# An AdaLN block with a Mamba scan and a mixture of experts: z of batch 0 in the y banks, the second norm's normalising step on ACT, and three groups of readout transposes at other places

## The reference

```
h  = layernorm(x) * (1 + ca) + sa
xz = h @ in_proj.T ;  xs, z = split(xz)                # 256 + 256 channels
u  = silu(causal_conv4(xs) + conv_b)
dt, Bm, Cm = split(u @ x_proj.T)                       # 8, 16, 16
delta = softplus(dt @ dt_w.T + dt_b)
h[t] = h[t-1] * exp(delta * A) + delta * u * Bm        # 16 states per channel
y    = sum_n h * Cm + u * D
x  = x + ga * ((y * silu(z)) @ out_proj.T)
h  = layernorm(x) * (1 + cb) + sb
x  = x + gb * (shared_expert(h) + top2_of_8_experts(h))  # gelu MLPs, 128 -> 256 -> 128
```

## Time and profile before

| | us |
|---|---|
| median of three executions | 722.49 |
| the profiled execution, its own time | 720.62 |
| its span, first to last instruction | 718.9 |
| PE busy | 612.3 (85%) |
| DVE busy | 583.7 (81%) |
| ACT busy | 496.8 (69%) |
| POOL busy | 322.4 (45%) |
| PE idle before L509, ended by ACT L821 | 15.8 |
| DVE idle before scans L1088, all | 28.1 |
| ACT idle before gelus L911, ended by PE L608 | 17.9 |

### The profile page before, as it was taken

How to read it: one execution, slowest core, us unless ns; L and a number is a source line. 1 busy time by engine, 2 the same in 40 slices (tenths; PEclk the granted TensorE clock), 3 DMA queues, 4 the chain that set the end, 5 groups by cost and what they waited for, 6 DMA issues and landing times.

```text
span 718.9 us, 9754 instructions
## 1 busy us (share of the span) xinstructions
PE 612.3 (85%) x3662; PEld 478.7 (67%) x3662; DVE 583.7 (81%) x669; ACT 496.8 (69%) x894; POOL 322.4 (45%) x172
## 2 busy tenths in 40 slices
PE   6637378999899999999999989999999858996797
PEld 4214255779566966778577956796687747795576
DVE  4494999989998999979997999899997999694300
ACT  2666742989578975899388947898399915871464
POOL 1043456445644555536543564455543654463000
PEclk9859559999999999999999999999999969997899
DMA  6413244313532244123431343223422243300000
GB/s 210 197 41 135 104 144 136 119 59 136 183 116 83 108 147 146 64 113 118 165 118 58 144 176 121 78 81 133 172 68 109 118 146 118 133 1 16 0 1 16
DMA packets 26369, 77.80 MB, mean 108 GB/s; under 512 B 2817, under 2 KB 17234, under 8 KB 18130
## 3 DMA queue, kind: packets, MB, share of 16 engines
q1 hardware_dynamic: 25842, 76.75, 29.7%
q10 hardware_dynamic: 480, 0.43, 0.2%
HBM read 74.55 MB, written 2.62 MB: 107 GB/s over the span
## 4 chain that ended last, share of the span: by engine, by line
PE 49%; ACT 23%; DVE 18%; issue 7%; POOL 2%; DMA 1%; DVEq 0%; POOLq 0%; ACTq 0%
PE psum L638 9%; PE psum L482 9%; DVE state L1088 9%; ACT decay L781 7%; PE psum L509 7%; ACT gT_mix L877 6%; DVE psum L1079 4%; PE psum L606 4%; PE psum L607 4%; PE psum L608 4%; ACT h L911 3%; PE psum L623 2%; PE psum L648 2%; PE psum L527 2%; POOL state L407 1%
## 5 line engine op out<-in xcount | busy, mean ns | idle before, releaser
L407 POOL TENSOR_TENSOR state<-state,bc 128x1024 f32<-128x1024 f32 x128 | 302.3, 2362 | 318.8 <-DVE psum L1079 317.7
L1088 DVE TENSOR_TENSOR_SCAN state<-decay,psum 128x1024 f32<-128x1024 f32 x128 | 292.2, 2283 | 28.1 <-PE psum L482 9.4
L781 ACT ACTIVATE decay<-delta,a_neg 128x511 f32<-128x511 f32 x256 | 166.9, 734 | 11.0 <-DVE state L1088 10.3
L482 PE MATMUL psum<-ident,state 128*128 128x128 f32 x1024 | 143.1, 288 | 31.3 <-POOL state L407 31.3
L482 PEld LDWEIGHTS psum<-ident,state 128*128 128x128 f32 x1024 | 124.4, 149 | 56.5 <-POOL state L407 41.7
L1079 DVE TENSOR_TENSOR psum<-bc,du 128x1024 f32<-128x1024 f32 x128 | 157.5, 1231 | 4.8 <-DVE state L1088 0.5
L638 PE MATMUL psum<-down_w,h 128*128 128x128 f32 x1024 | 125.3, 276 | 0.0
L638 PEld LDWEIGHTS psum<-down_w,h 128*128 128x128 f32 x1024 | 119.2, 192 | 6.1 <-issue 6.1
L911 ACT ACTIVATE h<-psum,vec 128x512 f32<-128x512 f32 x144 | 97.6, 688 | 19.1 <-PE psum L608 17.9
L877 ACT ACTIVATE gT_mix<-psum,w 128x128 f32<-128x128 f32 x256 | 74.6, 397 | 20.3 <-PE psum L648 12.9
L509 PE MATMUL psum<-h_sb,conv_in_wT 128*128 128x512 f32 x128 | 60.9, 623 | 15.8 <-ACT z_silu L821 15.8
(11 more groups left out here) (141 smaller groups left out, 621.9 us busy)
## 6 DMA issues: line engine op xcount, KB each, us to landing
bc<-bc_rows SPq DMA_DIRECT2D x64, 1024.0 KB, 4.8
x_sb<-_attn_hidden_states_dram SPq DMA_DIRECT2D x9, 256.0 KB, 2.8
out_dram<-out_sb SPq DMA_DIRECT2D x8, 256.0 KB, 2.4
x<-_attn_hidden_states_dram SPq DMA_DIRECT2D x7, 256.0 KB, 3.0
h<-in_L_ffn_rw_dram SPq DMA_DIRECT2D x1, 1024.0 KB
bc_rows<-rows SPq DMA_DIRECT2D x8, 64.0 KB, 3.6
h<-in_L_wmod_dram ACTq DMA_DIRECT2D x1, 384.0 KB
h<-in_L_attn_in_proj_w_dram SPq DMA_DIRECT2D x1, 256.0 KB, 4.6
```

Source lines behind the costliest of these rows:

```text
L407: pool.tensor_tensor(state[:, u % STATE_RING, :, :], state[:, u % STATE_RING, :, :], bc[:, pair % BC_RING, 1, first:first + NU, :], ALU.mu ...
L482: last = nc.tensor.matmul(Y[q][:, t * P:(t + 1) * P], state[:, u % STATE_RING, s, t * P:(t + 1) * P], ident[:, :], start=False, stop=(u in ...
L781: last = nc.scalar.activation(decay[:, r, s, 1:L], delta[:, b.p, q, 1:L], ACT.Exp, scale=a_neg[:, q, k:k + 1])
L1088: nc.vector.tensor_tensor_scan(state[:, u % STATE_RING, :, :].rearrange("p n t -> p (n t)"), decay[:, u % DECAY_RING, :, :].rearrange("p n ...
```

## The change

Six edits, in the order of the program:

1. z of batch 0 is computed in the prologue, into the banks Y (`z_bank`), around x_proj; its silu follows at once. It was computed into A after dt, and its silu stood at the end of slot 0's share before it, behind 12 decay instructions. The convolution of batch 1 now waits for softplus_abs of batch 0 where it waited for z's silu.
2. Still in front of slot 0, ACT's `h_rows` of batch 1 stands ahead of the decays of batch 0; in slot 0 PE runs y_start and y_add 0 ahead of x_proj.
3. `x1hat` goes from DVE to ACT: out = x * rstd + shift, by four activations. POOL makes shift = -mean * rstd in two more instructions of 128x4 behind make_rstd (`make_shift`).
4. On ACT, x1hat and h2_rows stand ahead of softplus_exp with its table load; they stood behind it.
5. The decays of unit 6 stand ahead of the silu table's load at the head of the slot; they stood behind h2_rows.
6. On PE, y_add 2 takes the place of seven of the twelve keep_busy transposes behind x1_transpose; y_add 3 stands behind the last up step, y_add 4 behind weights_transpose.

The rest is a constant of -1, a tile and two semaphores.

```diff
@@ -247,6 +250,10 @@

         block = ctx.enter_context(nc.Block())

+        def z_bank(n, half):
+
+            return Y[half] if n.i == 0 else A[half]
+
         def skip_rows(b):

             return gT_mix[:, :].rearrange("p (q t) -> p q t", q=Q) if b.i == 0 else skip
@@ -396,6 +404,14 @@
                 pool.wait_ge(eps_added, b.i + 1)
                 pool.tensor_tensor(rstd[:, which, :], rstd[:, which, :], minus_half,
                                    ALU.pow).then_inc(done, 1)
+
+            def make_shift(a):
+                pool.tensor_tensor(shift[:, :], mean_var[:, 1, :, 0], minus_one,
+                                   ALU.mult).then_inc(minus_mean, 1)
+                pool.wait_ge(minus_mean, a.i + 1)
+                pool.wait_ge(rstd2_done, a.i + 1)
+                pool.tensor_tensor(shift[:, :], shift[:, :], rstd[:, 1, :],
+                                   ALU.mult).then_inc(shift_done, 1)

             def readout(b, u, paced=True):
                 pair, q, first = unit(u)
@@ -416,6 +432,7 @@
                         readout(b, u)
                     if a and u == 2:
                         make_rstd(1, stats2_done, rstd2_eps, rstd2_done, a)
+                        make_shift(a)
                     if m and u == 5:
                         make_rstd(0, stats_done, rstd_eps, rstd_done, m)

@@ -463,6 +480,8 @@

                 if not (isinstance(b.i, int) and b.i == 0):
                     pe.wait_ge(gT_done, b.i)
+                else:
+                    pe.wait_ge(zs_done, 2)
                 pe.wait_ge(skip_done, Q * b.i + Q)
                 for q in range(Q):
                     for t in range(NT):
@@ -503,18 +522,24 @@
                     pe.wait_ge(h_done, n.i + 1)
                     if not (isinstance(n.i, int) and n.i < 3):
                         pe.wait_ge(mixmul_done, DOWNS * (n.i - 2))
-                    elif n.i > 0:
+                    elif n.i == 2:
                         pe.wait_ge(zs_done, 2 * n.i)
+                    elif n.i == 1:
+                        pe.wait_ge(sp_abs, Q)
                 for k in range(KC):
                     last = nc.tensor.matmul(A[q], conv_in_wT[:, q, k, :], h_sb[:, k:k + L],
                                             start=(k == 0), stop=(k == KC - 1))
                 last.then_inc(conv_done, 1)

             def z_proj(n, half):
-                pe.wait_ge(sp_abs, Q * n.i + half + 1)
+                if n.i > 0:
+                    pe.wait_ge(sp_abs, Q * n.i + half + 1)
+                else:
+                    pe.wait_ge(set_ev, EV_PROJ)
+                bank = z_bank(n, half)
                 for t in range(2):
                     rows_of = KC - 1 + (2 * half + t) * P
-                    last = nc.tensor.matmul(A[half][:, t * DI:(t + 1) * DI],
+                    last = nc.tensor.matmul(bank[:, t * DI:(t + 1) * DI],
                                             h_sb[:, rows_of:rows_of + P],
                                             z_wT[:, :], start=True, stop=True)
                 last.then_inc(z_done, 1)
@@ -668,13 +693,20 @@
                 if a:
                     y_add(a, UN - 3)
                     y_add(a, UN - 2)
+                if b and not a:
+                    y_start(b)
+                    y_add(b, 0)
+                if n and n.i == 0:
+                    z_proj(n, 0)
                 if n:
                     x_proj(n)
+                if n and n.i == 0:
+                    z_proj(n, 1)
                 if a:
                     y_add(a, UN - 1)
                 if a:
                     g_transpose(a, n)
-                if b:
+                if b and a:
                     y_start(b)
                 if a:
                     out_proj(a)
@@ -684,9 +716,9 @@
                     att_transpose(a)
                 if n:
                     dt_proj(n, 1)
-                if b:
+                if b and a:
                     y_add(b, 0)
-                if n:
+                if n and n.i > 0:
                     z_proj(n, 0)
                     z_proj(n, 1)
                 if b:
@@ -694,15 +726,20 @@
                 if a:
                     keep_busy(a, n, 14)
                     x1_transpose(a)
-                    keep_busy(a, n, 12)
+                if b:
+                    y_add(b, 2)
+                if a:
+                    keep_busy(a, n, 5 if b else 12)
                     router(a)
-                for k in range(M_UP):
-                    if a:
+                    for k in range(M_UP):
                         up(a, n, k)
-                    if b and k in (2, 8, 14):
-                        y_add(b, 2 + (k - 2) // 6)
+                if b:
+                    y_add(b, 3)
                 if a:
                     weights_transpose(a)
+                if b:
+                    y_add(b, 4)
+                if a:
                     shared_down(a)
                     down(a, 0)
                 if b:
@@ -812,14 +849,13 @@
                     nc.scalar.activation(skip_rows(n)[:, q, :], du[:, n.p, q, :], ACT.Identity,
                                          scale=vec[:, ROW_D + q:ROW_D + q + 1]).then_inc(skip_done, 1)

-            def z_gate(n):
-                if not (isinstance(n.i, int) and n.i < 2):
+            def z_gate(n, half):
+                if n.i >= 2:
                     act.wait_ge(gT_done, n.i - 1)
                 zs = z_silu[:, n.p, :, :].rearrange("p t c -> p (t c)")
-                for j in range(2):
-                    act.wait_ge(z_done, 2 * n.i + j + 1)
-                    nc.scalar.activation(zs[:, j * 512:(j + 1) * 512], A[j],
-                                         ACT.Silu).then_inc(zs_done, 1)
+                act.wait_ge(z_done, 2 * n.i + half + 1)
+                nc.scalar.activation(zs[:, half * 512:(half + 1) * 512], z_bank(n, half),
+                                     ACT.Silu).then_inc(zs_done, 1)

             def bcdt_rows(n):
                 act.wait_ge(xproj_done, n.i + 1)
@@ -884,6 +920,16 @@
                 nc.scalar.activation(turned[:, :], OUTP, ACT.Copy,
                                      scale=gateT[:, 1, bass.ds(a.i, 1)]).then_inc(acc_done, 1)

+            def x1hat(a):
+                act.wait_ge(shift_done, a.i + 1)
+                if a.i > 0:
+                    act.wait_ge(out_stored, 16 * a.i)
+                for t in range(NT):
+                    last = nc.scalar.activation(xhat2[:, t, :], residual_tile(a)[:, t, :],
+                                                ACT.Identity, scale=rstd[:, 1, t:t + 1],
+                                                bias=shift[:, t:t + 1])
+                last.then_inc(xhat2_done, 1)
+
             def h2_rows(a):
                 act.wait_ge(x1T_done, a.i + 1)
                 nc.scalar.activation(h2[:, :], MISC, ACT.Identity, scale=modT[:, 3, bass.ds(a.i, 1)],
@@ -912,11 +958,17 @@
                                      bias=vec[:, bias:bias + 1]).then_inc(gelu_done, 1)

             def slots(b, a, n, m):
+                if b:
+                    decays(b, AHEAD)
                 if n:
                     load_silu_table(n)
                     x_silu(n, 0)
                     x_silu(n, 1)
+                    if n.i == 0:
+                        z_gate(n, 0)
                     bcdt_rows(n)
+                    if n.i == 0:
+                        z_gate(n, 1)
                 if a:
                     g_rows(a, n)
                     att_rows(a)
@@ -925,14 +977,16 @@
                         softplus_relu(n, q)
                         softplus_abs(n, q, b)
                 if n and n.i > 0:
-                    z_gate(n)
+                    z_gate(n, 0)
+                    z_gate(n, 1)
+                if a:
+                    x1hat(a)
+                    h2_rows(a)
                 if n:
                     softplus_exp(n, a)
                 if a:
                     load_exp_table(a)
-                    h2_rows(a)
-                if b:
-                    decays(b, AHEAD)
+                if b:
                     decays(b, AHEAD + 1)
                 if a:
                     router_e(a)
@@ -945,6 +999,7 @@
                 if n and n.i == 0:
                     load_exp_table(n)
                     skip_term(n)
+                    h_rows(m)
                 if b:
                     decays(b, AHEAD + 2)
                 for j in range(DOWNS - 1):
@@ -954,7 +1009,7 @@
                         skip_term(n)
                     if n and j in (4, 5):
                         decays(n, j - 4)
-                    if m and j == 6:
+                    if m and j == 6 and m.i != 1:
                         h_rows(m)
                     if a:
                         mix_scaled(a, j)
@@ -966,8 +1021,6 @@
                 if n:
                     for u in range(3, AHEAD):
                         decays(n, u)
-                    if n.i == 0:
-                        z_gate(n)

             pipeline(act, slots, setup)

```

(14 more changed lines are left out.)

12 lines of the change are left out of this document (8 added, 4 removed).

## The result

The changed kernel took 717.58 us, the median of 20 runs (716.27 to 722.24), beside 721.59 of the kernel before (20 runs, 719.44 to 726.26). The ratio is 0.9946, 95% interval 0.9926 to 0.9965: faster by 0.5%, 3.9 us, where 12.4 were forecast (the medians are 4.0 apart). The profiled execution took 716.74 with a span of 715.0, beside 720.62 and 718.9.

What follows compares the result with a forecast made beforehand. It took the bound to be DVE's 9.44 us wait at the start, then slots racing PE, ACT and DVE. Span 718.9 - 9.1 - 0 - 3.8 + 0.5 = 706.5, median 710.1, range 703.5 to 716.

Steps and rivals of the forecast that it cites:

- The start: Up to the first gate_y: earlier convolution and y_add 0 remove DVE's wait; gain 9.1 us, bounds 5 and 9.4.
- Rival D: Start worth half: y_add 1 to 4 hold scans 5 to 8, 4.7 us returns; 719.5, no change; chance 0.04.
- ACT is free at 362.43: Middle slots: ACT is free before POOL's shift is there at 363.45, so x1hat does not wait for ACT.
- ACT's x1hat ... I take 1.15: Norm on ACT: four x1hat activations take 1.15 us, from four PSUM copies at 1.19; bounds 0.8 and 2.55.
- E's deciding point: Rival that x1hat on ACT is dear, deciding from 2.1 us for the four; 728.8, slower; chance 0.05.
- Falls of the clock at the up steps: PE idles 2.8 us before the fourth up step; clock falls in about four of six slots, 1.5 us each.
- Rivals B and C: Middle's clock stays up, 704.3, chance 0.17; or it falls in every slot, slot 7 too, 714.8, chance 0.17.
- The base: Slot lengths before the change: 76.8 us for the short kind, 1.53 more in slots 3, 4 and 5.
- Slot 7 and slot 8: Last two slots: slot 7 gains 3.8 us (bounds 2.2 and 4), slot 8 loses 0.5 (bounds 0 and 1.5).
- Rival F: Exp table load behind h2 stands behind a 1.28 us drain in six slots, losing 7.7; 717.8; chance 0.02.
- a trade at nothing: Slots 1 to 6: one lower-clock stretch traded for another, +4.8 us after against +4.6 before, so no gain.
- three signs of being wrong: First gate_y moves by less than 5.5 us, x1hat takes over 2 us, or all middle slots are below 76.

Runs made afterwards that it cites:

- after: The changed kernel with all six edits, against the kernel before: 717.58 us, ratio 0.995.
- e5: Changed kernel with x1hat back on DVE, h2_rows still ahead of softplus_exp: 709.86 us, 0.981 of the kernel before.
- e8: Changed kernel with x1hat's four activations lacking the bias operand, so the mean stays in (computation incomplete): one execution, 711.11 us.
- e6: Changed kernel with y_add 2 and 3 moved into PE's gap behind the third up step: 703.17 us, 0.976 of the kernel before.
- e4: Changed kernel with 22 useless transposes behind the third up step in slots 1 to 6: 709.59 us, 0.985 of the kernel before.
- e10: Changed kernel with ten useless transposes in PE's wait ahead of g_transpose, slots 1 to 6: 716.84 us, 0.994 of the kernel before.
- e2: Changed kernel with x1hat back on DVE and h2_rows behind the exp table again: 699.36 us, 0.971 of the kernel before.
- e1: Kernel before with only the start's edits (1 and 2), plus a third row of constants: 710.49 us, 0.987 of the kernel before.
- e3: Changed kernel with the y_adds back between the up steps (edit 6 undone): 715.97 us, 0.993 of the kernel before.
- e9: Changed kernel with edits 3, 4 and 5 undone, leaving the start's edits and the moved y_adds: 696.24 us, 0.967 of the kernel before.
- e12: Kernel before with only the y_adds moved (edit 6): 706.77 us, 0.980 of the kernel before.
- e11: Changed kernel with x1hat still on ACT, but x1hat and h2_rows behind softplus_exp again: 713.68 us, 0.990 of the kernel before.

## Why the prediction was wrong

**The start: right.** Each step came as told: 9.44 us of DVE's wait gone, the convolution near 36.9 (36.42), y_add 0 done near 48 (47.1), the first `gate_y` 9.1 earlier. The next wait, for y_add 1, had been put at nothing (0.7 us in hand); it is 0.38. Rival D fell.

**Slots 1 to 6: "ACT is free at 362.43" failed in five slots, and with it the silent step that PE is free for x1hat.** By these steps x1hat starts 12.58 us behind `gate_y` and the first gelu comes at 21.08. In slot 1 x1hat started at 12.55. In slots 2 to 6 the first gelu came at 22.20 to 22.25, since `z_proj` ran at the lower clock (2.69 to 3.43 us for 1.89), and two lists stand behind it. On ACT x1hat, behind z's second silu, started at 13.14 to 13.19 and ended at 14.78 to 14.83. On PE y_add 1 and fourteen keep_busy transposes follow, and PE came to x1_transpose at 14.88 to 14.93, without a pause. In after the two paths end within 0.1 us of each other, PE's last, and PE's doesn't depend on where x1hat is made: x1_transpose starts at 14.90 to 14.94 in the five late slots of e5, where x1hat on DVE had ended at 13.47, and at 14.92 in that of e8, where it had ended at 14.45. These five slots make 5.8 of the 6.3 us by which `gate_y` to the first gelu exceeds the forecast (132.8 against 126.5).

The prediction let the clock fall only at the up steps and put a fall at `z_proj` at nothing. The kernel before had one in slot 6: `z_proj` took 2.71 us, PE came to x1_transpose at 14.83, and the first gelu at 20.99 for 19.85.

**"ACT's x1hat ... I take 1.15" failed in size.** Four took 1.64. The nearest row was right in shape and wrong in operands; the bounds (0.8 to 2.55) held it. In slots 1 to 6 the 0.5 us shows in slot 1 alone (21.62 for 21.08); in the others the late `z_proj` hides it. With `z_proj` on time in all six it would have been 3 us, as e6's 21.6 in each slot has it. E's deciding point, 2.1 us, was not reached.

**Falls of the clock at the up steps: right in count, a little short in size.** I said a gap of 2.8 us ahead of the fourth up step and a fall in four of six slots; it was 2.6 and four (slots 1, 2, 4 and 6). e4 shows the mechanism. That the count was just four is partly luck: gaps of the same length were followed by a fall in three slots of five in e5, in three of six in e10 and in four of six in e8. Slot 6's fall cost 2.8 us, not 1.5: the clock stood at 0.50 from 525.4 to 531.6, about twice as long as in slot 4. The other three cost 1.3 to 1.5. Slot 3, without a fall, has 13.44 from the first gelu to the log table, beside 13.3 told. The 1.8 us by which the gelus exceed the forecast are 0.8 of this base in six slots and 0.9 of the falls. Rivals B and C fell.

**The base was off by 1.7 us.** I took slots 1 and 6 for the short kind of 76.8; they were 77.24 and 78.02 (in slot 6 by the late `z_proj`). This eased the error: 6.3 + 1.8 + 0.3 of small things less 1.7 is 6.7 of the 6.9 us.

**Slot 7 and slot 8** gave 1.1 less and 0.4 more than told. In slot 7 the first gelu, told 0.8 earlier than before, came 0.2 later (20.14 for 19.96 behind `gate_y`): x1hat ends at 14.47 there for 13.58 on DVE, 0.9 later. In slot 8 x1hat took 1.65 on ACT, 0.5 more than told:

```profile
666.74 1.65 ACT L928 ACTIVATE out_sb<-x_sb,shift,rstd 128x128 f32<-128x128 f32 x4 [4.69 <-POOL shift L413]
```

6.9 + 1.1 + 0.4 is 8.4 of the 8.5 us between the span told, 706.5, and the 715.0 measured.

**Rival F fell.** The exponential starts 0.02 us behind its table's load, 362.44 + 1.28 to 363.74, also in the new place. The rule of the Trainium skill ("ScalarE: Activation LUTs", section "What ACT_TABLE_LOAD costs") of a drain of some 1.38 us on top is again not what this trace shows.

**What I did not see.** The forecast called the middle a trade at nothing and did not ask which edits stood on which side. Edit 6 alone is worth 2.0%; edits 3 and 4 turn it and most of the start's gain back. They lengthen `gate_y` to the first gelu from 19.85 (e2) to 21.6 where `z_proj` is on time and 22.2 where it is late, and what this opens on PE is the gap. The working held both numbers, the 1.2 us that h2's new neighbours cost and the gap, but set them off against edit 6 instead of against leaving edits 3 and 4 out. None of my three signs of being wrong came (the first `gate_y` 9.1 earlier, x1hat at 1.64, no middle slot below 76): none of them covered `z_proj`.

**Open:** why `z_proj` falls to the lower clock. It does so in five slots of after and of e5, in six of e10, in three of e1, in two of e3 and e4, in one of e2, e9 and e12, in none of e6 and e11. The wait ahead of g_transpose is not it, and no run here shows what is. The rows show that it keeps step with the fall at the up steps: in after, e5 and e10 `z_proj` took 3.25 to 3.44 us in nine slots, and in each of them the clock fell behind the gap too; it took 2.69 to 2.75 in seven, and in none of them did it fall there. What a late `z_proj` costs can be read: with x1hat on DVE the first gelu then comes 21.1 behind `gate_y` for 19.85 (e1, e9, e12), with x1hat on ACT 22.2 for 21.6 (after, e4).

## What to carry to other kernels

Price an instruction that is new on an engine from a row with the same operands, not the same shape alone, and look whether what stands ahead of it is on time in every slot, not in the one you read, and on each engine that must be done before the next step: here the useless transposes behind a late `z_proj` held x1_transpose as much as x1hat did. When several edits meet in one stage, write down each one's sign: a sum near zero is a reason to measure them apart, and here the half (edits 1, 2 and 6) was six times the gain of the whole. Where an edit opens an idle stretch on TensorE, put work that must be done anyway into it.
